# Two fused transformer layers on one core: table rows, expert loads, last routing and final sums rearranged

## The reference

```python
# layer 0
x = x + relu(grouped_conv3x3(layernorm(x)) + bias)
h = softmax(layernorm(x) @ W_router)             # 32 experts
# each expert takes its 128 best tokens, and adds
# gate * (silu(tokens @ W_up[group]) @ W_down[expert]) to them
# layer 1
x = x + shifted_window_attention(layernorm(x))   # 16 heads, windows of 64
# each token takes its 2 best of 8 experts:
x = x + sum over the 2 of  weight * (silu(n @ w1.T) * (n @ w3.T)) @ w2.T,  n = layernorm(x)
```

## Time and profile before

| | us |
|---|---|
| median of 3 runs | 696.17 (695.05 to 698.48) |
| profiled execution | 700.56 |
| its span, first to last instruction | 698.6 |
| TensorE / VectorE / ScalarE / POOL busy | 475.7 / 377.3 / 376.4 / 350.6 |
| mean granted TensorE clock | 0.819 of full |

### The profile page before, as it was taken

How to read it: one execution, slowest core, us unless ns; L and a number is a source line. 1 busy time by engine, 2 the same in 40 slices (tenths; PEclk the granted TensorE clock), 3 DMA queues, 4 the chain that set the end, 5 groups by cost and what they waited for, 6 DMA issues and landing times.

```text
span 698.6 us, 13762 instructions
## 1 busy us (share of the span) xinstructions
PE 475.7 (68%) x4889; PEld 367.3 (53%) x4889; DVE 377.3 (54%) x1019; ACT 376.4 (54%) x800; POOL 350.6 (50%) x352
## 2 busy tenths in 40 slices
PE   4998521136557645158999998926998888888850
PEld 1354410012236434136777786505898878787750
DVE  4486578898111113389999999876122212212118
ACT  1487466518121212128777777321787777777635
POOL 3000000000777887266888887102777777777740
PEclk9999555558596877558999999765799999999985
DMA  9911352000254553610000000445111111111228
GB/s 313 354 32 47 93 118 96 0 0 0 53 150 100 141 117 31 209 44 2 3 3 3 2 4 2 127 86 162 50 50 50 50 50 50 53 48 54 50 74 321
DMA packets 40769, 55.77 MB, mean 80 GB/s; under 512 B 10464, under 2 KB 31008, under 8 KB 40320
## 3 DMA queue, kind: packets, MB, share of 16 engines
q1 hardware_dynamic: 29584, 40.64, 18.3%
q0 software_dynamic: 10688, 14.04, 9.6%
q10 hardware_dynamic: 432, 0.23, 0.1%
HBM read 34.99 MB, written 19.89 MB: 79 GB/s over the span
## 4 chain that ended last, share of the span: by engine, by line
POOL 29%; PE 21%; issue 16%; DVE 14%; DMA 10%; ACT 9%; POOLq 0%; DVEq 0%; SPq 0%; ACTq 0%
POOL arena L572 6%; POOL results L602 6%; POOL arena L594 5%; DMA arena<-normed,gather_i 4%; PE psum L1451 4%; PE psum L1423 4%; POOL scratch L516 3%; PE psum L1753 3%; ACT arena_b L1252 2%; POOL v_x L562 2%; PE psum L1737 2%; PE psum L1743 2%; POOL x_tok L555 2%; POOL x_tok L579 2%; ACT arena_b L1250 2%
## 5 line engine op out<-in xcount | busy, mean ns | idle before, releaser
L516 POOL DMA_INDIRECT scratch<-table,idx x32 | 33.7, 1052 | 179.1 <-DVE idx L873 169.6
L1154 DVE TENSOR_TENSOR arena<-arena,psum 128x384 f32<-128x384 f32 x71 | 39.4, 554 | 146.9 <-PE psum L1743 146.9
L594 POOL DMA_INDIRECT arena<-normed,gather_i x71 | 73.5, 1035 | 62.6 <-DVE gather_i L1130 41.3
L602 POOL DMA_INDIRECT results<-arena,dest_i x71 | 72.5, 1021 | 24.4 <-issue 16.3
L1423 PE MATMUL psum<-cst,arena 128*128 128x128 f32 x327 | 57.7, 290 | 29.7 <-DMA arena<-normed,gather_i 25.9
L572 POOL TENSOR_TENSOR arena<-arena,peak 128x1024 f32<-128x1024 f32 x32 | 60.9, 1902 | 25.5 <-DVE peak L985 25.5
L1370 ACT COPY arena_b<-w_sb 128x768 f32 x71 | 58.5, 824 | 23.1 <-issue 22.0
L1423 PEld LDWEIGHTS psum<-cst,arena 128*128 128x128 f32 x327 | 40.4, 146 | 38.3 <-DMA arena<-normed,gather_i 30.9
L1737 PE MATMUL psum<-arena,arena_b 128*128 128x128 f32 x426 | 60.5, 279 | 0.0
L1743 PE MATMUL psum<-arena,arena_b 128*128 128x128 f32 x426 | 60.3, 279 | 0.0
L1281 ACT ACTIVATE arena_b<-psum,bu_sb 128x512 f32<-128x512 f32 (+1 forms) x24 | 16.5, 686 | 80.2 <-PE psum L1566 80.2
(11 more groups left out here) (256 smaller groups left out, 1112.9 us busy)
## 6 DMA issues: line engine op xcount, KB each, us to landing
arena<-in_w_down_dram SPq DMA_DIRECT2D x8, 768.0 KB, 4.7
w_sb<-in_w_dram SPq DMA_DIRECT2D x3, 1536.0 KB, 15.4
y_odd<-zeros SPq DMA_DIRECT2D x4, 512.0 KB
table<-xn SPq DMA_DIRECT2D x8, 256.0 KB, 2.2
y_even<-x_tok SPq DMA_DIRECT2D x16, 128.0 KB
normed<-extra SPq DMA_DIRECT2D x8, 256.0 KB, 2.4
x_image<-x_tok SPq DMA_DIRECT2D x16, 128.0 KB
x_tok<-x_image SPq DMA_DIRECT2D x1, 2048.0 KB, 7.8
```

Of the source, the lines that this page charges most:

```text
L516: nc.gpsimd.indirect_dma_start(out=rows_b[:, e // 4 % 4, e % 4, :], out_offset=None, in_=table[:, :], in_offset=bass.IndirectOffsetOnAxis( ...
L594: nc.gpsimd.indirect_dma_start(out=rows_d[:, t % ROWS_D, :], out_offset=None, in_=normed[:, :], in_offset=bass.IndirectOffsetOnAxis(ap=gat ...
L602: nc.gpsimd.indirect_dma_start(out=results[:, :], out_offset=bass.IndirectOffsetOnAxis(ap=dest_i[:, t:t + 1], axis=0), in_=yx_d[:, t % OUT ...
L1154: nc.vector.tensor_tensor(act_d[:, b, :], silu_d[:, b, :], psum[:, 4 + b, 0:FF_D], ALU.mult).then_inc(e_act, 1)
```

## The change

- The normed rows of block n go to tiles 4n to 4n+3 of `extra`, a buffer of all 32 tiles, in place of `xn[:, 1]`. `norm_b` no longer waits for the transposes or the table.
- The logits' second half uses PSUM bank 0. VectorE takes both halves out after its pipeline; `first_logits` and its semaphore are gone. TensorE's block 4 waits for the last convolution's partial sums instead.
- ScalarE makes a dummy exponential before the last `evac_b`.
- The zeros of `y_odd` are written after `y_even`. The last layer's expert weights (`LATE_LOADS`) are loaded after the gates' table columns, and ScalarE waits for them before the last experts.
- The last routing's top two are found for tiles 0 to 15 and then for tiles 16 to 31. `gate_rows(0)` stands before five set-up instructions of VectorE, and `gate_back(0)` one block earlier on TensorE.
- The last of the four one-hot runs is made in two parts of eight columns.
- In the tail, blocks 2, 4 and 6 are combined on TensorE: VectorE makes 24 diagonal matrices of the weights (`diag_f`) after its last product, TensorE multiplies them with the two results of each tile and adds both in PSUM (banks 1 to 3), and VectorE adds that to `x_tok` in one instruction. The blocks end in the order 0, 1, 3, 2, 5, 4, 7, 6.

```diff
+PARTS_D = [(r, 0, COLS_D) for r in range(RUNS_D - 1)] + [(RUNS_D - 1, 0, COLS_D // 2), (RUNS_D - 1, COLS_D // 2, COLS_D)]
+ENDS_F = (0, 1, 3, 2, 5, 4, 7, 6)
+ON_PE_F = (2, 4, 6)
...
+        diag_f, _ = shared(w13_sb[:].rearrange("p e k h -> p (e k h)"), 0, [P, len(ON_PE_F), 4, 2, P])
...
-            sp.wait_ge(s_zero, 1)
-            for c in range(4):
-                sp.dma_start(y_odd.rearrange("(p line) c -> p (line c)", p=P)[:, 1024 * c:1024 * (c + 1)],
-                             zeros[:]).then_inc(b_init, 16)
...
-                sp.dma_start(tab_v[:, 4 * n:4 * n + 4, 0:P], xn[:, 1]).then_inc(b_tab, 16)
+                sp.dma_start(tab_v[:, 4 * n:4 * n + 4, 0:P], extra[:, 4 * n:4 * n + 4, :]).then_inc(b_tab, 16)
...
+            for dst, src in LATE_LOADS:
+                sp.dma_start(dst, src).then_inc(ld_late, 16)
...
+            dve.wait_ge(ld_w, 16 * len(LOADS))
+            dve.wait_ge(s_zero, 1)
             minus_top(0)
...
+            gate_rows(0)
             nc.vector.tensor_scalar(before_b[:], C("tri"), -1.0, None, ALU.add)
...
+            link(gate_logits(0))
+            top_two(0)
             gate_rows(1)
             link(gate_logits(1))
+            top_two(1)
...
+            for n, (r, a, b) in enumerate(PARTS_D):
+                of_tile, of_lane = [P, TILES_D, b - a], [P, P, b - a]
...
+                nc.vector.tensor_tensor(oh_lane[:, r, :, a:b], lane_h[:, :, a:b],
+                                        slot_lane[:, r:r + 1, a:b].to_broadcast(of_lane), ALU.is_equal)
...
+            dve.wait_ge(e_w, RUN_D)
+            for m, n in enumerate(ON_PE_F):
+                for j in range(4):
+                    for k in range(2):
+                        ins = nc.vector.tensor_scalar(diag_f[:, m, j, k, :], ident, weights_i[:, k, 4 * n + j:4 * n + j + 1],
+                                                      None, ALU.mult)
+                ins.then_inc(f_diag, 1)
...
+                if n in ON_PE_F:
+                    m = ON_PE_F.index(n)
+                    dve.wait_ge(f_mixed, m + 1)
+                    nc.vector.tensor_tensor(x_tok[:, tiles, :], psum[:, 1 + m, :].rearrange("p (t c) -> p t c", c=P),
+                                            x_tok[:, tiles, :], ALU.add).then_inc(f_sum, 1)
+                    continue
...
             def evac_b(n):
+                if n == BLOCKS - 1:
+                    nc.scalar.activation(peak1[:, 0:1], std[:, 0:1], ACT.Exp)
...
                 act.wait_ge(b_rs, n + 1)
-                if n > 0:
-                    act.wait_ge(b_tr, n)
-                    act.wait_ge(b_tab, 16 * n)
...
-                if n >= BLOCKS // 2:
-                    pe.wait_ge(b_first, 1)
+                if n == BLOCKS // 2:
+                    pe.wait_ge(a_part, 4 * BLOCKS)
...
+            pe.wait_ge(e_silu, RUN_D)
+            for m, n in enumerate(ON_PE_F):
+                pe.wait_ge(f_diag, m + 1)
+                pe.wait_ge(f_back[n], 16 * 2)
+                for j in range(4):
+                    for k, back in enumerate((back1, back2)):
+                        ins = nc.tensor.matmul(psum[:, 1 + m, P * j:P * (j + 1)], diag_f[:, m, j, k, :],
+                                               back[:, 4 * n + j, :], start=k == 0, stop=k == 1)
+                ins.then_inc(f_mixed, 1)
```

More of the change, by code:

```diff
@@ L455, in _ @@
                     sp.dma_start(y_windows[r, w], x_tok[at:at + 8]).then_inc(b_init, 16)
+            sp.wait_ge(s_zero, 1)
+            for c in range(4):
+                sp.dma_start(y_odd.rearrange("(p line) c -> p (line c)", p=P)[:, 1024 * c:1024 * (c + 1)],
+                             zeros[:]).then_inc(b_init, 16)
             sp.wait_ge(b_gate, 2)
@@ L499, in _ @@
                                  results_v[k, :, 4 * n:4 * n + 4, :]).then_inc(f_back[n], 16)
-            for n in range(BLOCKS):
-                sp.wait_ge(f_sum, n + 1)
+            for at, n in enumerate(ENDS_F):
+                sp.wait_ge(f_sum, at + 1)
                 sp.dma_start(out_v[:, 4 * n:4 * n + 4, :], x_tok[:, 4 * n:4 * n + 4, :]).then_inc(done, 16)
@@ L1045, in _, with gate_rows, gate_logits, best @@
             first, second = pick[:, 0], pick[:, 1]
+            def gate_rows(h):
+                dve.wait_ge(d_log, (4, BLOCKS + 1)[h])
+                nc.vector.tensor_copy(xn[:, h].rearrange("p k n -> p (k n)"), psum[:, (2, 5)[h], :]).then_inc(d_rows, 1)
+            def gate_logits(h):
+                dve.wait_ge(d_log, (BLOCKS - 2, BLOCKS + 2)[h])
+                return nc.vector.tensor_copy(
+                    lg[:, 16 * h:16 * h + 16, :].rearrange("p (n k) e -> p n k e", k=4),
+                    psum[:, 6 + h, :].rearrange("p (k n e) -> p n k e", k=4, n=4)[:, :, :, 0:EXPERTS_D])
+            def best(h, of, top_of, onehot):
+                tiles = slice(16 * h, 16 * h + 16)
+                rank_h = rank8[:, tiles, :]
+                link(nc.vector.tensor_reduce(top_of[:, tiles], of[:, tiles, :], AX.X, ALU.max))
+                link(nc.vector.tensor_tensor(hit[:, tiles, :], of[:, tiles, :], wide(top_of[:])[:, tiles, :], ALU.is_equal))
+                link(nc.vector.tensor_tensor(hit[:, tiles, :], hit[:, tiles, :], rank_h, ALU.mult))
+                link(nc.vector.tensor_reduce(rank[:, tiles], hit[:, tiles, :], AX.X, ALU.max))
+                link(nc.vector.tensor_tensor(onehot[:, tiles, :], rank_h, wide(rank[:])[:, tiles, :], ALU.is_equal))
+            def top_two(h):
+                tiles = slice(16 * h, 16 * h + 16)
+                best(h, lg[:], peak1, first)
+                link(nc.vector.scalar_tensor_tensor(lg[:, tiles, :], first[:, tiles, :], -3.0e38, lg[:, tiles, :],
+                                                    ALU.mult, ALU.add))
+                best(h, lg[:], peak2, second)
+            gate_rows(0)
             nc.vector.tensor_scalar(before_b[:], C("tri"), -1.0, None, ALU.add)
@@ L1413, in _ @@
             act.wait_ge(d_xback, 16 * 2)
-            for n in range(BLOCKS):
+            for n in ENDS_F:
+                if n in ON_PE_F:
+                    continue
                 act.wait_ge(f_back[n], 16 * 2)
@@ L1699, in _ @@
                              start=True, stop=True).then_inc(d_wi, 1)
-            for r in range(RUNS_D):
-                k, first_run = r * 2 // RUNS_D, r % (RUNS_D // 2) == 0
-                pe.wait_ge(d_col, r + 1)
-                for c in range(COLS_D):
+            for n, (r, a, b) in enumerate(PARTS_D):
+                k, half_run = r * 2 // RUNS_D, r % (RUNS_D // 2)
+                pe.wait_ge(d_col, n + 1)
+                for c in range(a, b):
                     ins = nc.tensor.matmul(psum[:, 4, TILES_D * k:TILES_D * (k + 1)], oh_lane[:, r, :, c],
-                                           oh_token[:, r, :, c], start=first_run and c == 0,
-                                           stop=not first_run and c == COLS_D - 1)
+                                           oh_token[:, r, :, c], start=half_run == 0 and c == 0,
+                                           stop=half_run == RUNS_D // 2 - 1 and c == COLS_D - 1)
             ins.then_inc(d_inv, 1)
```

78 lines of the change are left out of this document (27 added, 51 removed).

## The result

The changed kernel took **692.55 us** (median of 19 runs, 690.69 to 697.51). The kernel before, run beside it, took 700.16 (19 runs, 695.05 to 705.49). The ratio is 0.9911, with a 95% interval from 0.9889 to 0.9933: faster by 6.2 us, 4.7 to 7.8. That is under 1%, and clear of its own interval. The forecast was a saving of 5.3 and a time of 690.9, so the saving was 0.9 short by the ratio (2.3 by the medians) and the time 1.65 low. The base was the largest error: the 696.17 from which the saving was taken is the median of three runs, and 19 runs gave 700.16. The measured ratio on that base of 696.17 would be 690.0.

What follows compares the result with a forecast made beforehand. No single engine bounds the kernel (none passes 68% busy); stages are limited by chains of waits. Savings 3.9 + 0.55 + 0.15 + 1.3 - 0.6 = 5.3 us off 696.17 gave 690.9 us, range 688.8 to 693.4 (forecast's own 689.8 to 692.0).

Steps and rivals of the forecast that it cites:

- The base: Starting time for the whole kernel: 696.17 us, median of three timed runs, from which the 5.3 us saving was taken.
- First stage: End of the first stage: 3.9 us saved, 3.0 of it from ScalarE rounds of 3.2 us; ends 3.0 and 4.5.
- the table load: Exp table load on ScalarE, moved before the first stage's last copy: about 1 us of that stage's saving.
- Loads: Weight loads and zeros moved later on SP's queue: 0 us, as nothing before 175 us waits for them.
- Routing halves: Last routing on VectorE, by halves: 0.55 us saved, eleven steps of 0.325 us per half; ends 0 and 1.0.
- Split run: Last one-hot run in two parts: 0.15 us saved, only TensorE's idle 0.16 us goes; lower end a 1.4 loss.
- loses its packed form: Rival, split one-hot run: each part costs a whole run, 1.4 us lost for 0.15 saved; 692.4 us, chance 0.07.
- Scatters: POOL's last three scatters beside VectorE's diagonals: 0.2 us lost each, 0.6 in all; ends 0.3 and 6.3.
- POOL is shut out: Rival, last three scatters: POOL gets nothing until the diagonals end, 6.3 us lost instead of 0.6; 696.6 us, chance 0.08.
- Tail: Final sums and writes: 1.3 us saved, the end set by the last read's landing plus eight DMA writes of 5.3 us.
- TensorE stays slow to the end: Rival, tail: diagonal sums stay at 3.4 us a block, saving 0.25 us instead of 1.3; 692.0 us, chance 0.15.
- First stage only sheds its writes: Rival, first stage: round near 3.5 us and last copy fully delayed, saving 1.8 us; 693.0 us, chance 0.10.

Runs made afterwards that it cites:

- warm: Changed kernel plus 24 TensorE matmuls of 128x512 in its wait before the diagonal sums; 698.83 us (10 runs), ratio 0.9997 to the kernel before.
- rows_old: Changed kernel with normed rows of every block back in one place, the norm waiting for transposes and table write; 698.04 us, ratio 0.9973 to the kernel before.
- exp_late: Changed kernel without the dummy exponential before the last copy, so the table load is where it was; 693.57 us, ratio 0.9928 to the kernel before.
- long_train: Changed kernel plus five unused VectorE copies of 128x2048 ahead of the diagonals, over the last three scatters; 695.12 us (one run).
- warm2: Changed kernel plus twelve TensorE matmuls of 128x512, ending before the first diagonal sums; 694.21 us (5 runs), ratio 0.9908 to the kernel before.
- the reordering: Changed kernel with ScalarE, in the first stage's last rounds, norming a block before copying the previous block's transposes; 691.44 us, ratio 0.9887 to the kernel before.

## Why the prediction was right or wrong

**The base: wrong.** The step that failed is the first one, "I take the saving off the median": it took 5.3 off 696.17, and the kernel before takes 700.2. Of 68 further runs of it, 19 lie at or under 698.5, where all three shown runs lay, and their median is 700.3. That the first three all lay there was bad luck (about one in fifty, an estimate from 19 in 68), but a median of three invites it. That the lowest of the three lay 1.1 under their median told nothing of the spread upward. The profiled execution, at 700.56, was nearer to the truth than their median, and I had set it aside. The interval I gave took the spread for the lower end alone (and there 689.7 - 1.1 is 688.6, not 688.8). So 692.55 stands above the forecast's own range of 689.8 to 692.0. That it is only 1.65 off is luck: the base was 4.0 too low, and the saving 0.9 to 2.3 too small. From the right base the forecast would have been 700.2 - 5.3 = 694.9, 2.35 too high.

**The saving: right in direction and place, with terms mis-sized.** By the distances, the rounds of the first stage gave 3.43 for 3.0, the scatters lost 0.1 to 0.2 for 0.6, the split run gave 0.37 for 0.15, and the tail 1.0 for 1.3.

**First stage: mechanism right, 0.45 short.** 3.9 forecast, 4.35 measured. The norm of the last block came 3.43 sooner where I had 3.0: 0.71 for 0.56 at block 4, and then rounds of 3.09, 2.88 and 3.33 for 3.2, as the clock was full through most of them (transposes 0.67 at 65.1, and 1.13 only from 67.99). Where the clock fell later, in the variant warm, the third round was 3.12 and the norm came 0.2 sooner still (15.01). Behind the norm the table load gave 0.92 for 1. The two parts add up: rows_old shows the table load's part without the place per block, exp_late the place per block without the load. The second logits bank by itself was not tried; exp_late leaves nothing for it.

**Loads: right, 0.** **Routing halves: right**, 0.6 for 0.55, with the step at 0.323 and the second half's row copy 0.9 us later, as forecast (27.31 us after the last attention block instead of 26.41).

**Split run: right in kind, 0.37 for 0.15.** I had counted only TensorE's idle gap. In the rows after, VectorE's last part ends at 472.39 and TensorE 1.78 later, instead of 2.43; VectorE pays 2 x 1.46 - 2.60 = 0.32 for that. The difference, 0.33, is near the 0.37. Told from TensorE's side, two runs of 16 matmuls took 2.44 and 2.41 us with 0.16 between them, 5.01 in all, and 32 in one go take 4.65: besides the 0.16, some 0.2 that a run loses at its ends. The rival "loses its packed form" fell, as each part costs 1.46. No run isolates the term.

**Scatters: 0.1 to 0.2 for 0.6.** The mis-sized term was 0.2 for each of three; a scatter lost 0.00 to 0.09. It took the loss of a gather beside 0.2 us operations and doubled it, with a diagonal at 0.27 us which took 0.21. The rival "POOL is shut out" fell, and long_train shows the same beside longer operations: each scatter loses at most one copy, and ends inside the train.

**Tail: right, 1.0 for 1.3**, and by the argument given: DMA's writes set it. The last read lands 14.47 us after the first is issued and the last write at 19.60, so eight writes take 5.1 us where I had 5.3; in the kernel before VectorE was the limit, whose last sum ended at 18.6. The missing 0.3 fits the last read, which landed 0.4 later than before (14.04). The rival "TensorE stays slow to the end" fell (the rise came at 682). What it would have cost was not measured: warm2 tells only that sums at the full clock bring next to nothing.

**First stage only sheds its writes: fell**; the round is 2.9 to 3.3.

## What to carry to other kernels

Three runs of a kernel are a poor base for an absolute time; forecast the saving, and let the range hold the base's own spread on both sides. Compare traces by distances between fixed points of the program and over several profiles, since the first pair here overstated the gain by 3.6 us, most of it luck with the clock. Put a fixed point between two parts of a change as well: the whole stretch hid 0.9 us of gain behind one slow write. When a wait is taken away, look for the next longest round and for what shares a buffer with the work that is moved: here the reordering gained 0.6 us at the last norm, and the copy that stood behind it took 0.5 back.

## What was not expected of the hardware

A dip of TensorE's clock at 18 us (granted 0.66 to 0.73 between 17 and 22 us, that is the lower of its two levels, 1.2 GHz, for more than half of the time) came in 8 of 13 profiles of nearly the same program, and cost 1.6 us in one block and about 2.3 in the first two together (14.3 to 15.4 us with the dip, 12.4 to 12.9 without). The stretch from the index operation to the first experts' sums, which no variant touches, took 114.5 to 116.8 us. Between them these cover much of the 7 us by which runs of one kernel differ. What causes either is open.
